# A graph network's setup on one Trainium2 core: the last five tiles of x loaded second, their statistics moved in between the one-hots of a histogram

## The reference

```python
def _layernorm(x, axis=-1, eps=1e-05):
    m = jnp.mean(x, axis=axis, keepdims=True)
    v = jnp.var(x, axis=axis, keepdims=True)
    return (x - m) / jnp.sqrt(v + eps)

def gcn_conv(x, edge_index, W, b, n_nodes):
    ...
    deg = jax.ops.segment_sum(jnp.ones(src.shape, x.dtype), dst, num_segments=n_nodes)
    dinv = jnp.where(deg > 0, jax.lax.rsqrt(deg), jnp.zeros_like(deg))
    norm = dinv[src] * dinv[dst]
    h = x @ W.T
    msg = h[src] * norm[:, None]
    out = jax.ops.segment_sum(msg, dst, num_segments=n_nodes)
    return out + b

edge_index = jnp.stack([src, dst])
h = jnp.maximum(_layernorm(x, axis=-1), 0.0)
x = x + _L0_gnn_ref(h, edge_index, L0_gnn_W1, L0_gnn_b1, L0_gnn_W2, L0_gnn_b2)
h = jnp.maximum(_layernorm(x, axis=-1), 0.0)
x = x + _L1_gnn_ref(h, L1_gnn_W_fc, L1_gnn_attn_l, L1_gnn_attn_r, L1_gnn_W_res, src, dst)
```

## Time and profile before

| | |
|---|---|
| time, median of 3 runs | 1844.84 us (1842.23 to 1847.53) |
| the profiled execution | 1838.35 us, its span 1836.5 us |
| granted TensorE clock over the span | 0.89; 1.00 up to 100 us |
| busy: PE, DVE, ACT, POOL | 1317.4, 1094.9, 759.4, 1236.2 us |
| the setup block | from 0 to about 96 us |
| first gather of the first convolution | 100.55 us |

### The profile page before, as it was taken

One profiled execution on the slowest core, in us unless ns is written; L12 is line 12 of the kernel. 1 busy time (PEld: TensorE's weight loads), 2 busy tenths in 40 slices (PEclk: granted clock), 3 DMA queues, 4 the chain that ended last, 5 costly groups with the idle time before them and its releaser, 6 DMA issues. The chain is left out here.

```text
span 1836.5 us, 43411 instructions
## 1 busy us (share of the span) xinstructions
PE 1317.4 (72%) x13383; PEld 855.2 (47%) x13384; DVE 1094.9 (60%) x1947; ACT 759.4 (41%) x2383; POOL 1236.2 (67%) x1297
## 2 busy tenths in 40 slices
PE   6357777778777857888788888872676676666665
PEld 4224444444444534555555555541454444444443
DVE  7724444445444524555555555543888888888886
ACT  6601111111111111222222222223788888888885
POOL 3167777777777457777777777607777777777760
PEclk9978899899989978999999999986878888888887
DMA  9679999999999669999999999919999999999991
GB/s 266 245 253 333 353 349 337 329 333 336 333 331 331 230 237 333 363 356 371 370 362 358 352 363 372 335 66 330 314 339 347 345 350 347 355 352 346 351 315 61
DMA packets 139994, 585.27 MB, mean 319 GB/s; under 512 B 30615, under 2 KB 32751, under 8 KB 139945
## 3 DMA queue, kind: packets, MB, share of 16 engines
q0 software_dynamic: 100272, 497.49, 75.7%
q1 hardware_dynamic: 32563, 67.72, 10.7%
q10 hardware_dynamic: 7110, 19.43, 2.8%
HBM read 534.42 MB, written 50.12 MB: 318 GB/s over the span
## 5 line engine op out<-in xcount | busy, mean ns | idle before, releaser
L704 POOL DMA_INDIRECT ring_c<-table,slot_c x834 | 795.7, 954 | 307.0 <-issue 286.9
L1202 POOL DMA_INDIRECT ring<-table,slot x417 | 414.7, 995 | 140.5 <-issue 116.3
L757 ACT ACTIVATE slot_c<-units 128x8 int32 (+1 forms) x104 | 21.7, 210 | 790.6 <-DMA ring_c<-table,slot_c 738.4
L1347 ACT ACTIVATE ring<-ring,weight x1152 | 279.0, 336 | 0.6
L1609 DVE TENSOR_TENSOR ring<-ring,ps_w 128x3120 f32 x72 | 242.7, 3399 | 18.0 <-ACT ps_w L1327 18.0
L1451 PE MATMUL ps_acc<-ring,hot_f 128*32 128x195 f32 x3136 | 178.3, 375 | 87.2 <-DVE ring L1609 86.0
L956 DVE TENSOR_TENSOR hots<-iota,units 128x256 f32<-128x256 bf16 x102 | 42.9, 428 | 301.6 <-PE ps_sum0a L904 118.4
L899 PE MATMUL ps_yb<-weights,sum_tb 128*128 128x512 f32 (+1 forms) x576 | 193.3, 492 | 2.9 <-ACT weights L791 0.8
L899 PE MATMUL ps_ya<-weights,sum_ta 128*128 128x512 f32 (+1 forms) x576 | 189.9, 486 | 0.0
L1451 PEld LDWEIGHTS ps_acc<-ring,hot_f 128*32 128x32 f32 x3136 | 105.2, 123 | 148.4 <-DVE ring L1609 111.1
L899 PEld LDWEIGHTS ps_yb<-weights,sum_tb 128*128 128x128 f32 x576 | 108.1, 191 | 84.0 <-issue 71.1
(11 more groups left out here) (296 smaller groups left out, 1950.6 us busy)
## 6 DMA issues: line engine op xcount, KB each, us to landing
ring_c<-table,slot_c POOLq DMA_INDIRECT x834
table<-weights SPq DMA_DIRECT2D x25, 396.0 KB, 5.3
table<-nodes SPq DMA_DIRECT2D x25, 384.0 KB
table<-nodes ACTq DMA_DIRECT2D x25, 384.0 KB, 5.4
turned_table<-weights SPq DMA_DIRECT2D x25, 384.0 KB
nodes<-in_x ACTq DMA_DIRECT2D x24, 384.0 KB
turned_g<-turned_table SPq DMA_DIRECT2D x24, 384.0 KB
out_x<-nodes SPq DMA_DIRECT2D x24, 384.0 KB
```

What stands on the lines that cost most here:

```text
L704: eng.indirect_dma_start(out=ring[:, t * QH + k, :], out_offset=None, in_=table, in_offset=bass.IndirectOffsetOnAxis(ap=slot[t][:, k:k + 1 ...
L757: eng.activation(slot[t][:, :], units[:, ds(q, 1), t * QH:(t + 1) * QH + t].rearrange("p a c -> p (a c)"), ACT.Copy).then_inc(slot_ready[t ...
L1202: eng.indirect_dma_start(out=ring[:, b * RB + at * FROW:b * RB + (at + 1) * FROW], out_offset=None, in_=table3, in_offset=bass.IndirectOff ...
L1347: last = eng.activation(head, head, ACT.Copy, scale=weight[:, c, h:h + 1])
```

## The change

Two places of the setup are written differently. SP loads the last group of x, with its two transfers, right behind group 0, so that groups 1, 2 and 3 come behind it. On DVE the fourteen steps of one-hots are split: four stay in the loop, the last ten are written out, and one `bn_stats` of the last group stands behind each of them. The wait for the last group's semaphore moves from behind the histogram to in front of the fifth step. Nothing is computed otherwise.

```diff
-                    for g in range(NT // XG):
+                    for g in [0, NT // XG - 1] + list(range(1, NT // XG - 1)):
                         r0, r1 = g * XG * P, min((g + 1) * XG * P, N)
                         full = (r1 - r0) // P
                         eng.dma_start(nodes[:, g * XG:g * XG + full, :], x[r0:r0 + full * P, :].rearrange("(t p) d -> p t d", p=P)).then_inc(s_x[g], 16)
...
-                    with eng.Fori(0, HCOLS // HSTEP // 2) as i:
+                    def make_hots(i, par):
+                        eng.wait_ge(s_hdone, i * 2 + par + 1)
+                        for hot_, numbers, n, given in ((lo_hot, lo_iota, PH, lo), (hi_hot, hi_iota, 2 * NT, hi)):
+                            eng.tensor_tensor(...).then_inc(s_lo, 1)
+                    turns = HCOLS // HSTEP // 2
+                    with eng.Fori(0, turns - XG) as i:
                         for par in range(2):
-                            eng.wait_ge(s_hdone, i * 2 + par + 1)
-                            for hot_, numbers, n, given in ((lo_hot, lo_iota, PH, lo), (hi_hot, hi_iota, 2 * NT, hi)):
-                                eng.tensor_tensor(...).then_inc(s_lo, 1)
+                            make_hots(i, par)
                     eng.wait_ge(s_x[NT // XG - 1], 32)
                     for j in range(XG):
                         for h in range(2):
+                            make_hots(turns - XG + j, h)
                             last = eng.bn_stats(stats[:, j, h, :], nodes[:, NA + j, h * D // 2:(h + 1) * D // 2])
                     link(last)
```

More of the change, by code:

```diff
@@ L353, in _ @@
                     eng.wait_ge(s_pool, POOL)
-                    with eng.Fori(0, HCOLS // HSTEP // 2) as i:
+                    def make_hots(i, par):
+                        eng.wait_ge(s_hdone, i * 2 + par + 1)
+                        for hot_, numbers, n, given in ((lo_hot, lo_iota, PH, lo), (hi_hot, hi_iota, 2 * NT, hi)):
+                            eng.tensor_tensor(hot_[:, par, :, :, :], numbers[:, :, :].unsqueeze(1).to_broadcast([P, 2, n, HPAIR]),
+                                              given[:, ds((i * 2 + par) * HSTEP, HSTEP)].rearrange("p (a k) -> p a k", a=2).unsqueeze(2).to_broadcast([P, 2, n, HPAIR]), ALU.is_equal).then_inc(s_lo, 1)
+                    turns = HCOLS // HSTEP // 2
+                    with eng.Fori(0, turns - XG) as i:
                         for par in range(2):
-                            eng.wait_ge(s_hdone, i * 2 + par + 1)
-                            for hot_, numbers, n, given in ((lo_hot, lo_iota, PH, lo), (hi_hot, hi_iota, 2 * NT, hi)):
-                                eng.tensor_tensor(hot_[:, par, :, :, :], numbers[:, :, :].unsqueeze(1).to_broadcast([P, 2, n, HPAIR]),
-                                                  given[:, ds((i * 2 + par) * HSTEP, HSTEP)].rearrange("p (a k) -> p a k", a=2).unsqueeze(2).to_broadcast([P, 2, n, HPAIR]), ALU.is_equal).then_inc(s_lo, 1)
+                            make_hots(i, par)
                     eng.wait_ge(s_x[NT // XG - 1], 32)
```

## The result

The changed kernel takes 1851.11 us in the median of 5 runs (1850.53 to 1854.60), the kernel before 1844.84 us (5 runs, 1842.23 to 1849.22). The ratio is 1.0036, 95% interval 1.0018 to 1.0053, so 6.3 us slower where I had forecast 3.0. The profiled execution takes 1851.11 us, its span is 1849.3.

What follows compares the result with a forecast made beforehand. The setup, a chain ending on DVE before the first gather at 100.55 us, was taken as the bound. ACT's 5.3 us wait less 2.3 of slack adds 3.0 to the 1844.84 us median: 1847.8 us, range 1842 to 1852.

Steps and rivals of the forecast that it cites:

- DVE's edit costs nothing and is worth 1.5 us: Setup, DVE: ten bn_stats fit the 0.71 us gaps between one-hot steps; places could be copied 1.5 us earlier.
- The 53 rows lie on one engine: Setup, loads of x: the last group's 53-row transfer (159 KB) runs on a single DMA engine, not spread over 16.
- the rival of spread rows: Setup loads: the 53 rows are spread, ACT does not wait, 1.5 us faster, 1843.3 us; chance 0.10.
- that of a delay given back before the gather: Setup end: something else ends the setup, so the delay vanishes before the first gather, 1844.8 us; chance 0.05.
- Whole tiles at 19.6: Setup loads: the last group's four whole tiles take 3.9 us behind group 0 and land at 19.6 us.
- ACT's slack 2.3 us: Setup, before DVE's reciprocal of the degrees' root: ACT's chain could run 2.2 to 2.3 us later without delaying it.
- One engine's pace: Setup loads: 0.122 us a row, 6.5 us for the 53 rows, landing at 26.1 us; group 1 at 31.0.
- DVE's wait before the fifth step: Setup, one-hots: DVE wants the last group at 24.33 us, gets it at 26.1; histogram ends 1.2 us later.
- Group 2 at 35.9 ... both are there.: Setup, ACT's statistics: group 2 lands at 35.9, group 3 at 40.8 us, before ACT wants them; no second wait.
- The 3.0 us: End of setup: ACT's 5.3 us wait for group 1 less 2.3 us of slack makes it 3.0 us later.
- The rival of the slow lone engine: Setup loads: 0.34 us a row, 18 us for the rows, setup 14.5 us later, 1859.3 us; chance 0.05.
- Its threshold, 0.17 us a row: Setup loads: from this pace, 9 us for the 53 rows, the loss passes 0.3% (5.5 us).

Runs made afterwards that it cites:

- the rows alone: Changed kernel with nothing else in flight while the 53 rows load (SP waits before and behind them); not timed, first gather at 107.49 us.
- the split: Changed kernel with the 53 rows loaded as 48 and 5; ratio 0.998 to the kernel before, 1.0002 when timed again.
- the 37: Changed kernel with the 53 rows loaded as 37 and 16; no time given, first gather at 104.76 us.
- the run without the weights: Changed kernel with the four loads of weights issued only when group 3 of x has landed; no time given, first gather at 105.59 us.

## Why the prediction was right in kind and short in size

- **DVE's edit costs nothing and is worth 1.5 us.** Right: 0.23 us of idle time is left in each step, and without the waits for x the places come 1.67 us and the first gather 1.6 us earlier.
- **The 53 rows lie on one engine.** Right, shown by the rows alone (share 0.06), by the split (no waits) and by the 37 (a shorter wait). With it fall the rival of spread rows and that of a delay given back before the gather.
- **Whole tiles at 19.6, ACT's slack 2.3 us.** Right: 19.56 in the run where it can be seen; ACT's waits of 8.37 + 2.59 less 2.3 are 8.7, against the 8.5 by which the first gather moved.
- **"One engine's pace": 53 x 0.122 = 6.5 us, group 1 at 31.0.** Too short; this is the term that failed. The rows landed at 28.5 instead of 26.1, about 8.9 us behind the whole tiles, and group 1 at 34.1, 5.6 us later where I had 4.9 and where the run without the weights had 4.8. I took the pace of a full stream and of an engine alone, and neither holds for an engine that works off a load of its own beside 15 others. The slow pace had been in the profile only at the weights (144 GB/s), which I put aside as a rival. DVE's wait before the fifth step rested on the same term: the histogram was 3.9 us late, not 1.2.
- **"Group 2 at 35.9 ... both are there."** Wrong: it landed at 45.6, and ACT waited 2.59 us more. The lone engine was then still at x while others had begun the weights. Holding these back removed the wait.
- **The 3.0 us.** It was 8.5 in the setup, where the first gather came at 109.03 and not near 103.5, and 6.3, 12.1 and 10.4 in the three pairs of medians. The sum of ACT's waits, 5.3 predicted, was 10.96. The rival of the slow lone engine named this mechanism at 0.34 us a row for all rows; half of that was true. Its threshold, 0.17 us a row, is just what the rows cost on the average, and the second wait came on top.
- **The range and the chances.** That 1851.11 lies inside 1842 to 1852 is partly luck: the 8.5 us of the setup on 1844.84 give 1853.3, and the later timings put the loss higher still. I had given 0.86 to a time that can't be told from before and 0.11 to a slower one; the interval, 1.0018 to 1.0053, lies above 1, so the less likely case came.
- **Its rule.** The split of 125 partitions on five engines and of 53 on one, which I drew from the Trainium skill ("DMA: Bandwidth & Descriptors", "Why a DMA increments its semaphore by 16 and not by 1"), agrees with every run here, with 37, 48 and 80 partitions too.

## What to carry to other kernels

Before a load is moved ahead of others, look at how evenly it lies on the DMA engines: a tail where the share of busy engines is one or five of 16 shows that some load lies unevenly, which may be harmless only because it comes last, as here. Loads behind it land when its slowest engine is through, and the engines beside it can make that engine slower still. Cutting such a remainder so that its bulk divides by 16, as 48 and 5 here, costs one more issue.

## What the runs showed that I had not expected

- An engine that alone holds a load moves 25 GB/s by itself, 0.12 us for a row of 3 KB. The 53 rows cost it about 0.17 us each on the average beside 15 others at 128-partition tiles, and its part of group 2 (40 rows in 11.4 us) 0.28 us a row while they load pieces over 32 partitions. The total falls too, from 402 to 355 and 141 GB/s, at a share of busy engines of 1.
- The same program took 1845 us on one chip and 2371 and 2367 us on two others, at a granted clock of 0.89 and 0.82. The setup, at a clock of 1.00 on all of them, was equally long. The clock is 8% lower and the time 28% longer, so the clock by itself does not account for it; what else differs stays open.
